# Causal and full self-attention of a four-layer decoder in one streamed form, fed by hi/lo stacks of head pairs

## The reference

```python
def _L1_attn_ref(x, Wq, bq, Wk, bk, Wv, bv, Wo, bo):       # causal
    ...
    scores = jnp.einsum('bhqd,bhkd->bhqk', q, k) / math.sqrt(hd)
    causal = jnp.tril(jnp.ones((s, s), dtype=bool))
    scores = jnp.where(causal[None, None], scores, jnp.asarray(-10000.0, scores.dtype))
    probs = jax.nn.softmax(scores, axis=-1)
    ctx = jnp.einsum('bhqk,bhkd->bhqd', probs, v)
    ...
    return ctx @ Wo + bo

def _L2_attn_ref(x, Wq, Wk, Wv, W_out, b_out):             # full, no mask
    ...
    energy = jnp.einsum('bqhd,bkhd->bhqk', q, k) / jnp.sqrt(jnp.float32(e))
    attn = jax.nn.softmax(energy, axis=-1)
    out = jnp.einsum('bhqk,bkhd->bqhd', attn, v).reshape(b, s, e)
    return out @ W_out.T + b_out

x = _layernorm(x + _L1_attn_ref(x, ...), axis=-1)          # L1a
...
x = _layernorm(x + _L2_attn_ref(x, ...), axis=-1)          # L2a
```

## Time and profile before

| | us |
|---|---|
| median of 3 runs | 3257.47 (3252.22 to 3268.54) |
| the profiled execution, its own time | 3278.77 |
| its span | 3277.0 |
| L1a from its first projection to its first step | 544.6 to 612.7 |
| L1a steps | 612.7 to 978.7 |
| L2a from its first projection to its first step | 1549.1 to 1663 |
| L2a steps | 1663 to 2050.7 |

### The profile page before, as it was taken

How to read it: one execution, slowest core, us unless ns; L and a number is a source line. 1 busy time by engine, 2 the same in 40 slices (tenths; PEclk the granted TensorE clock), 3 DMA queues, 4 the chain that set the end, 5 groups by cost and what they waited for, 6 DMA issues and landing times. The chain is left out here.

```text
span 3277.0 us, 40639 instructions
## 1 busy us (share of the span) xinstructions
PE 2589.0 (79%) x15232; PEld 1634.8 (50%) x15232; DVE 1627.7 (50%) x3177; ACT 1118.9 (34%) x1890; POOL 822.6 (25%) x795
## 2 busy tenths in 40 slices
PE   0143089999999889996898999867889889589993
PEld 0133066444434357994343332435666543379992
DVE  6716963555545532224578884546634454441115
ACT  4212022344444321111146567331144333214441
POOL 7385900011120101331200000011214521025551
PEclk9957589999999879997779889967999899669996
DMA  3012100000000021994301210003200000139995
GB/s 130 14 63 80 61 1 23 2 1 2 2 3 19 2 103 61 333 330 161 58 9 32 40 20 1 8 11 92 89 5 2 20 18 2 55 127 353 352 348 189
DMA packets 72030, 264.02 MB, mean 81 GB/s; under 512 B 18016, under 2 KB 35192, under 8 KB 53523
## 3 DMA queue, kind: packets, MB, share of 16 engines
q1 hardware_dynamic: 56282, 227.65, 20.5%
q0 software_dynamic: 15552, 33.78, 3.1%
HBM read 226.24 MB, written 21.83 MB: 76 GB/s over the span
## 5 line engine op out<-in xcount | busy, mean ns | idle before, releaser
L1827 DVE TENSOR_REDUCE cmax<-max_ps 128x1 f32<-128x512 f32 x512 | 319.0, 682 | 80.3 <-PE max_ps L1706 80.3
L2447 PE MATMUL A<-xbT,w 128*128 128x128 f32 x2512 | 302.3, 277 | 0.7 <-DMA w<-L1f_W_dram 0.3
L1803 ACT ACTIVATE prob<-st_ps 128x1024 f32<-128x1024 f32 x256 | 247.6, 1021 | 139.1 <-PE st_ps L1720 138.6
L2447 PEld LDWEIGHTS A<-xbT,w 128*128 128x128 f32 x2512 | 292.0, 193 | 1.7 <-issue 1.0
L1017 PE MATMUL ring<-kT,qT 32*128 32x192 f32 (+4 forms) x1280 | 287.0, 461 | 3.9 <-ACT qT L1097 1.1
L1148 DVE TENSOR_REDUCE cmax<-ring 128x1 f32<-128x512 f32 (+3 forms) x416 | 204.2, 529 | 170.7 <-PE ring L1025 123.4
L1127 ACT ACTIVATE prob<-st_ps 128x1024 f32<-128x1024 f32 (+5 forms) x256 | 203.9, 803 | 233.7 <-PE st_ps L1005 232.9
L1706 PE MATMUL max_ps<-kst,qst 48*128 48x512 f32 x512 | 206.5, 517 | 41.4 <-DVE cmax L1827 21.4
L1005 PE MATMUL st_ps<-qT,kT 32*128 32x512 f32 (+5 forms) x1344 | 233.1, 455 | 0.6 <-ACT prob L1127 0.4
L952 POOL TENSOR_SCALAR_AFFINE_SELECT prob<-prob 128x512 f32<-128x512 f32 (+1 forms) x200 | 121.5, 608 | 441.5 <-ACT prob L1127 434.4
L2458 PE MATMUL C<-w,hid 128*128 128x256 f32 x944 | 223.0, 380 | 0.0
(11 more groups left out here) (397 smaller groups left out, 4830.6 us busy)
## 6 DMA issues: line engine op xcount, KB each, us to landing
w<-L3f_W_dram SPq DMA_DIRECT2D x79, 1026.0 KB
w<-L1f_W_dram SPq DMA_DIRECT2D x39, 1536.0 KB
down_coef<-L0f_down_coef_dram SPq DMA_DIRECT2D x10, 1024.0 KB, 4.9
coef_u<-L0f_up_coef_dram SPq DMA_DIRECT2D x10, 1024.0 KB, 4.8
gate<-L2f_gates_dram SPq DMA_DIRECT2D x6, 1536.0 KB, 8.4
room<-y_rows_dram SPq DMA_DIRECT2D x4, 2048.0 KB, 10.6
qst<-qp SPq DMA_DIRECT2D x96, 64.0 KB, 2.4
raw<-L2f_W_dram SPq DMA_DIRECT2D x12, 384.0 KB, 9.2
```

What stands on the lines that cost most here:

```text
L1803: act.activation(prob[:, g % 2, 2 * p:2 * p + 2, 0:hi - lo], st_ps[0:kp, p, :, 0:hi - lo], ACT.Exp, scale=scale).then_inc(s.exp_done, 1)
L1827: dve.tensor_reduce(cmax[:, first:first + len(pairs), tiles[0]:tiles[0] + len(tiles), part], max_ps[:, e % MAXB, :].rearrange("p (a c n) - ...
L2447: mm = pe.matmul(A[:, j % 2 * 2 + a, f * TB:(f + 1) * TB], up_w(w[:, j % WB], a, k, f), xbT[:, j % 2, k, :], start=(k == 0), stop=(k == KT ...
```

## The change

A function `stacked_attention` replaces `self_attention` for L1a and `paired_attention` for L2a. It keeps the streamed form of `self_attention` (two groups a step, values two steps behind, three `prob` buffers, POOL dividing by the sums) and takes the stacks of `paired_attention`.

- Scores and pieces are fp32r products of 48 rows (pieces) or 64 rows (scores), two heads at a time.
- `parts` holds hi and lo of q and k of one group of 8 heads (two units). ACT reads each projection twice, once into `parts` as hi, once into `raw` as f32; POOL subtracts. SP copies the stacks of each unit with 24 DMAs; for unit 0 POOL issues 12 of them.
- Projections are made per group of 8 heads: 4 of 512 tokens for q and k, 2 for values with 8 small products each, between the chunks of the group before. Before, L1a projected per unit of 4 heads.
- `LEAD` is 10 chunks for both kinds (12 in L1a, 1.25 units of 16 tiles in L2a before).
- The maxima go to the queries per half and by two DMAs of the SP queue (before: one DMA of SP per half in L1a, two of POOL per unit in L2a).
- The weights of L1a come in three plain loads instead of two padded ones.

```diff
+def stacked_attention(nc, env, dram, kind, scale, w_count, ahead=None):
+    RING = 3
+    SLOTS = 3
+    PROBS = 3
+    LAG = 2
...
+    LEAD = 10
+    HP = 3 * HD
+    COPIES = 3 * HU
+    GROUPS = N // 2
...
+    splits = [(what, k, half) for k in range(GROUPS) for what in ("keys", "queries") for half in range(HALVES)]
+    def projections_due(c):
+        g, i = divmod(c, nC)
+        items = []
+        for x in range(4):
+            if g % 2 == 0 and g // 2 + 1 < GROUPS and i == nC // 2 + x * (nC // 2) // 4:
+                items.append(splits[4 * (g // 2 + 1) + x])
+        for x in range(2):
+            if i == nC // 3 + x and (g == 0 or g % 2 and g // 2 + 1 < GROUPS):
+                items.append(("values", (g + 1) // 2, x))
+        return items
...
+            @block.sync
+            def _(sp):
+                def stack(g):
+                    u = units[g][1]
+                    if g >= SLOTS:
+                        sp.wait_ge(s.s_ready, 2 * nS * (g - SLOTS + 1))
+                    else:
+                        sp.wait_ge(s.q_cleared, g + 1)
+                        sp.wait_ge(s.k_cleared, g + 1)
+                    sp.wait_ge(s.split, 4 * (g // 2 + 1))
+                    for h in range(HU):
+                        at, row = 64 * (h % 2), (u % 2 * HU + h) * HD
+                        for r, part in enumerate((0, 0, 1)):
+                            sp.dma_start(qst[at + r * HD:at + (r + 1) * HD, g % SLOTS, h // 2, :].bitcast(F32),
+                                         parts[row:row + HD, 1, part, :].bitcast(F32)).then_inc(stacked[g % SLOTS], 16)
+                    if g:
+                        copy_keys(sp, g, stacked[g % SLOTS])
...
+                stack(0)
...
+                for g in range(N):
+                    if g + 1 < N:
+                        stack(g + 1)
+                    for half in range(HALVES):
+                        n = g * HALVES + half
+                        sp.wait_ge(*freed_of(("turn", n)))
+                        for p in range(2):
+                            sp.dma_start(qst[HP:P:64, g % SLOTS, p, half * CH:(half + 1) * CH].bitcast(F32),
+                                         crow[2 * TH * p:2 * TH * (p + 1), n % 2, :].bitcast(F32)).then_inc(c_loaded[half], 16)
...
+            @block.tensor
...
+                def group(step, p, c):
...
+                    for side in range(2 if pack else 0):
+                        j, lo, hi, _ = pack[0]
+                        rows = slice(64 * side, 64 * (side + 1))
+                        mm = pe.matmul(st_ps[:, p, side, 0:hi - lo], kst[rows, g % SLOTS, p, j * P:(j + 1) * P], qst[rows, g % SLOTS, p, lo:hi],
+                                       start=True, stop=True, skip_group_check=True)
...
+                        rows = slice(64 * side, 64 * side + HP)
+                        mm = pe.matmul(spot(key)[:, 0:k1 - k0], qst[rows, gm % SLOTS, 1 - p, t * P:(t + 1) * P],
+                                       kst[rows, gm % SLOTS, 1 - p, k0:k1], start=True, stop=(not masked), skip_group_check=True)
...
+            @block.scalar
+            def _(act):
+                def keep(what, k, half):
...
+                    act.activation(parts[:, which, 0, half * CH:(half + 1) * CH], spot(key), ACT.Identity, bias=bias_of)
+                    act.activation(raw[:, n % 2, :], spot(key), ACT.Identity, bias=bias_of).then_inc(s.act_freed, 1)
...
-                self_attention(nc, env, group("L1a_"), "causal", float(HD ** -0.5), self_weights(more), 32,
-                               ahead=cross_weights("L1x_", wx[:, :]))
...
+                stacked_attention(nc, env, group("L1a_"), "causal", float(HD ** -0.5), 48, ahead=cross_weights("L1x_", wx[:, :]))
...
-            paired_attention(nc, env, group("L2a_"), float(D ** -0.5), 96, ahead=cross_weights("L2x_", wx))
+            stacked_attention(nc, env, group("L2a_"), "full", float(D ** -0.5), 112, ahead=cross_weights("L2x_", wx))
```

More of the change, by code:

```diff
@@ L35 @@
 STACK = 4 * HD
-STAGES = 5
+STAGES = 6
 TAGS = []
@@ L2717, in weights_of, with layer0 @@
             return load
-        def layer0(more):
+        def layer0():
             with ExitStack() as ws:
@@ L2725, in layer0 @@
                 wide_cross(nc, env, space("L0x_"), down_stages(nc, weights, down, NS // 2, NS - NS // 2))
-                butterfly_ffn(nc, env, space("L0f_"), down, self_weights_of("L1a_", more))
+                butterfly_ffn(nc, env, space("L0f_"), down, weights_of("L1a_"))
         def cross_weights(prefix, to):
@@ L2772, in masks @@
                     return load, make
-                self_attention(nc, env, group("L3a_"), "window", float(HD ** -0.5), self_weights(more), 144, masks=masks)
+                self_attention(nc, env, group("L3a_"), "window", float(HD ** -0.5), self_weights(more), 160, masks=masks)
                 mask = named(qk=staticmethod(lambda b, t: seen_qk[:, b, t, :]), kq=staticmethod(lambda b, lo, hi: seen_kq[:, b, lo:hi]))
-                cross_attention(nc, env, group("L3x_"), "xmask", HD, float(HD ** -0.5), wx[:, :], 160, mask)
-        def first_layers():
-            with ExitStack() as ws:
-                more = sbuf(nc, ws, "more", [P, d["L1a_W2"].shape[1]])
-                with nc.cleanup_on_exit():
-                    layer0(more)
-                with nc.cleanup_on_exit():
-                    first_attentions(more)
+                cross_attention(nc, env, group("L3x_"), "xmask", HD, float(HD ** -0.5), wx[:, :], 176, mask)
         def last_layers():
@@ L2845, in paired_rows @@
         return c(w.reshape(NU // 2, 2, HU, HD, -1).swapaxes(1, 2).reshape(w.shape))
-    r["L1a_bv"], r["L1a_bo"] = a["L1_attn_bv"], a["L1_attn_bo"]
+    for n in ("Wq", "Wk", "Wv", "bv", "bo"):
+        r["L1a_" + n] = a["L1_attn_" + n]
+    for n in ("bq", "bk"):
+        r["L1a_" + n] = columns(a["L1_attn_" + n])
     r["L1a_Wo"] = paired_rows(a["L1_attn_Wo"])
@@ L2871, in cross_weights @@
         return c(np.concatenate(parts + [columns(quads(bq, hd)), columns(ones)], -1))
-    r["L1a_W"], r["L1a_W2"] = self_weights(*(a["L1_attn_" + n] for n in ("Wq", "Wk", "Wv", "bq", "bk")))
     none = np.zeros(D, a["L3_attn_Wq"].dtype)
```

725 lines of the change are left out of this document (381 added, 344 removed).

## The result

| | before | after |
|---|---|---|
| median, us | 3261.48 (3252.22 to 3268.54, 4 runs) | 3174.64 (3169.88 to 3176.43, 4 runs) |
| span of the profiled execution, us | 3277.0 | 3172.6 |
| ratio of times, 95% interval | 1 | 0.9733 [0.9704, 0.9762] |

The change is faster by 87 us between medians and by 104 us between the traces: the traced execution of before took 3278.8 us, 17 more than its median, that of after 3174.4, its median. I forecast 151 less, a time of 3106 us, with a range of 3050 to 3200.

The account below looks back on a forecast made before the run. PE was taken to pace the L1a steps and DVE the L2a steps. L1a opening -9, L1a steps -101, L2a opening -51 and L2a steps +10 gave -151 from a median of 3257.5: 3106 us, range 3050 to 3200.

Parts of the forecast that it names:

- fp32r groups: L1a steps: a full group of two scores and two pieces falls from 1.08 to 0.58 us, saving 9.0 a unit.
- in the full steps DVE's 2.68 exceeds what PE needs: L1a full steps: DVE's 2.68 us against PE's 2.15; units go from 48.2 to 34.5 us, steps to 265.
- L1a projections: L1a steps: 15 items at 1.95 us, 4.1 us a unit against 9 before, saving 4.9.
- L1a clock: L1a steps: PE taken at full clock, as in all L1a steps before, with no time added for half clock.
- L1a opening: Before the L1a steps: first piece after 27 us, then ten chunks paced by DVE in 31; 9 us less.
- L2a opening: Before the L2a steps: the same 27 us chain, then ten chunks and three items in 35; 51 us less.
- L2a steps: L2a units of 51.1 us: DVE 43.5, waits 3.2, projections 3.0, late maxima 1.4; 398 against 387.7, +10.
- DVE alone: Rival, chance 0.21: DVE sets both stages, L1a at 31 and L2a at 47 us a unit; 3051 us.
- Late feed: Rival, chance 0.18: maxima's DMAs wait behind SP's copies, 2.5 us more for each of 32 halves; 3186 us.
- Clock falls: Rival, chance 0.05: PE's clock falls to half in both stages; at a share of 55%, 3303 us.

Follow-up runs that it names:

- plain f32 kernel: The changed kernel with its scores and pieces over the same stacks read as plain f32 in place of fp32r; 3560.94 us, one run.
- Half maxima: The changed kernel with each maximum taken over half of its columns only, the other half left out; 3116.63 us, one run.
- divided values: The changed kernel with each step's values in two halves of 256 columns, the second behind the second group; 3151.03 us, ratio 0.9637.
- divided values and undivided closes: The kernel with divided values, but with the values in one piece at the last step of each half; 3131.42 us, ratio 0.9572.
- filler ahead of the opening: The kernel with divided values except at closes, plus 24 extra products behind each attention stage's first four projections; 3138.22 us beside 3131.77.
- quarter: The changed kernel with later groups' projections cut to one of two products, expected as a quarter of each item; 3150.11 us, one run.

## Why the prediction was right or wrong

- **L1a steps, fp32r groups** (1.08 to 0.58 us): right in size. A pair takes 0.35 us and a second pair behind it 0.23 (871.30, 871.65, 871.88), about as in the earlier trace rows. The plain f32 kernel shows that it is the type.
- **L1a steps, "in the full steps DVE's 2.68 exceeds what PE needs", unit 34.5 us**: this is the step that failed. The 34.5 is PE's work of before less the savings, 34.3, with 0.2 for waits, and DVE's 2.68 was the reason to add no more. But 2.68 was no limit of DVE; it was the period of a loop in the paired form, where pieces are issued ahead of scores. The stacked form issues scores first, and a full step takes 2.94. A unit without projections takes 33.9 and not 30.4: 3.5 x 7.17 = 25 us. Half maxima and divided values each moved the full step in the way that the loop says, and brought this unit to 31.1 and 31.4. So 2.5 to 2.8 of the 3.5 are waits of the loop, and the rest is PE's own work, which I had 0.7 to 1.0 too short.
- **L1a projections**: 1.95 each was too much. (40.18 - 33.88) / 4 with the unit 737.99 to 778.17, which has four at full clock, and (36.92 - 33.88) / 2 give 1.6 and 1.5: 6 us less than forecast for the 15 items.
- **L1a clock**: taken as full. Spells at 0.50 (617 to 634, 665 to 675, 784 to 794) cost about 12 us, by the units with and without one: 42.4 - 36.9, 42.6 - 40.2 and 40.4 - 36.9, in all 11.5. 25 - 6 + 12 = 31, the miss. One more spell, 887 to 893, lies in the last ten steps, which took 21 us from the last negation on where I had 18, and the first two chunks took 3 us less than a sixth of a unit and their item. In the 5 us ahead of the four spells PE is busy 3.9 to 4.2 and its longest wait is 0.7 us, so a gap like the one of 1.86 us that I read in the earlier trace rows is not what stood ahead of them.
- **L1a opening** (59): the first piece was right, forecast and measured 27 us after the start. The ten chunks took 40 us where I had 31. "Paced by DVE" failed there: DVE is busy 24.5 of those 40, PE is at clock 0.50 for the first 18 and once more for 3, and five projections hold PE for about 2 us each at full clock. What each of these costs was not separated.
- **L2a opening** (-51): right, -54. The first piece comes 26 us after the start (27 forecast), and the opening shrinks from 113.9 to 59.8.
- **L2a steps** (+10): 20 measured. Projections at 1.3 each were right (1.41 and 1.34). A unit without any takes 48.9, by two halves of 24.46, against 43.5 + 3.2 + 1.4 = 48.1, but by other parts: DVE works 42.4 and waits 6.5, mostly in the 0.46 us of nine full steps and not for late maxima. That the sum came near is luck, since both its parts were off. It is 6 us in 7.375 units; the tail of ten steps took 22.8 and not 21, and the clock was still at 0.50 for the first 5 us.
- **The rivals.** DVE alone: no; it is busy 316 of 408 in L2a and 198 of 296 in L1a. It became true only in the L2a of the kernel with divided values and undivided closes, where DVE is busy 42.8 of 44.0 us without projections, while PE is busy 31.1 of 31.4 in L1a. In that L2a the rule of the Trainium skill (TensorEngine Tiling (Array Packing), section PSUM Bottleneck) fits: with faster products the reading of PSUM bounds, 2.49 us a full step beside DVE's 2.48. In the changed kernel it was neither engine but the passage through the three banks between them; another number of banks was not run. Late feed: no; scores wait 0.22 to 0.32 us for the row of maxima at a half, 4.7 us in the whole kernel. Clock falls: in part, in L1a alone (0.92 over its steps), while L2a rose from 0.90 to 0.99.

The median moved by 87 us, and I had 151. Of the 64 us between, 46 are these misses, and 17 come from the traced execution of before, which lay above the median that I subtracted from. That the pieces ahead of the scores would win the 0.27 back in the stacked form is argued from these rows and was not run.

## What to carry to other kernels

When two engines hand work over through a few banks, read a period as a loop: follow one bank from its release through everything that stands in the queue until the next release. A busy share of 90% on an engine in such a loop is not its limit, and a step time taken over from another form holds only with the same order of issue. To shorten the loop, divide the longest piece between two fills, and keep together what runs side by side. And when an experiment leaves work out, count in its trace how much: here a "quarter" was a half, which turns the reading round.

## What the runs showed of the hardware

- Products in four column strips overlapped as neighbours in the queue and not across another product. Eight f32 records of four heads take 1.07 us; with one 48-row product between the second and the third head, each four records take 1.05.
- A product of 48 or 64 rows and 512 columns takes two records in f32 and one in fp32r. A pair in two row strips takes 0.86 to 0.96 and about 0.34 us.
- Halving the columns of a sum of eight records (1.00 to 0.57 us) costs 0.14 us a step, and gave back more than it cost in all but the closing steps.
- The clock read 0.50 in stretches of 10 and 17 us (617 to 634, 665 to 675) whose records show PE busy throughout, and a filler ahead of the opening moved its fall by 20 us and gained no time.
- Twelve copies of 64 KB take SP 7.6 us to issue alone and 11.7 beside twelve of POOL.
